# A graph layer with an on-chip sort: the first layer's exponential taken in two ScalarE passes, and four smaller moves

## The chip, the cores and the metric

The kernel runs on one core of a Trainium2 chip. The metric is the device time of one execution in microseconds (us). Three runs of the kernel before took 552.17, 550.02 and 552.18 us; their median is 552.17 us.

## The reference

`x` is 50,000 nodes by 128 features, with 12,500 edges (`src`, `dst`, 128 attributes each), all float32.

```python
edge_sum = segment_sum(edge_attr, src, 50000)
inputs   = concatenate([x, edge_sum], axis=1)        # 256 wide
h = elu(inputs @ W0 + b0)
h = elu(h @ W2 + b2)
out = h @ W3 + b3
return layernorm(x + out)                            # no scale, no shift
```

Only nodes that are the source of an edge have a nonzero `edge_sum`. The second half of `W0` matters for them alone.

## The kernel before, in words

**Items.** The nodes are worked on in 124 items, four blocks of up to 128 columns each. 98 dense items take all nodes in order (512 columns) as if they had no edges. 25 edge items (500 columns) and a last one (100) compute again the nodes that have edges, and their rows are scattered over the dense rows in `out`. Items 0 to 49 are dense, then one edge item and two dense ones take turns; the last six items are dense 118, edge 119 (group 23), dense 120 and 121, edge 122 (group 24) and the last one, 123.

**Steps.** Each engine's program is written out by hand as one loop over steps c = 0, 1, 2, ...; an engine runs its own list in order and waits on semaphores. In step c the engines work on several items at once:

- TensorE (PE): `layer1` of item c-1 (line 600, into `l1_ps`), `layer2` of item c-3 (L636), `layer3` of item c-5 (L646 and L647, eight products into one of three `z_ps`). `layer3` waits until the item three before it has left `z_ps`.
- ScalarE (ACT): `exp` of item c-1 (L720, `e1`), `turned`, which copies item c-1's x with a bias into `xT` (L713), `exp` of item c-3 (L720, `e2`), `squares` of item c-5 (L733, eight instructions), and for the second item of each pair in `ROOTS` a logarithm and an exponential that give `seed` (L741, L743).
- VectorE (DVE): `scale` (three small instructions on the root of a pair, L989 to L994), `first_layer` (the elu of item c-1), `output` (L1011, the normalised rows, seven steps after an item's number), `second_layer` (the elu of item c-3, L978 and L980).
- SyncE (SP) loads x and stores dense rows; GpSimd (POOL) issues the indirect DMAs: 100 that fetch x rows by edge (L441), 100 that gather edges in sorted order (L451), 100 that scatter edge rows (L470) and one for the last item (L494).

**The sort.** In steps 1 to 31 VectorE also sorts the edges by source: a bitonic network on a 128 by 128 tile `net`, in 31 groups of 2 to 5 operations, one group a step (`sort_group`). A compare is two instructions (L869, L870). Fourteen groups begin with the tile turned over by TensorE (`turn_net`, L532); these are steps 8, 9, 11, 12, 14, 15, 17, 18, 20, 22, 24, 26, 28 and 30, called turned steps here. `turn_net` waits for the last operation of the group before (`net_done`), and the group's first operation waits for the turned tile. The function `run(parts, beside)` deals the group's operations out between the step's parts: part, piece beside, part, piece beside, and what is left at the end.

**The bias on TensorE.** In steps 4 to 31 (`fused`) a third product (`add_bias`, L585) adds b0 + 1 to `l1_ps`, from three bf16 rows of b0 + 1 (`bias_rows`) against a row of ones. VectorE then needs one instruction for the elu, L974, `max(min(e1, 1), l1_ps)`, instead of two (L978, L980). The rows are made in steps 2 and 3 by `split_b0` (VectorE, from L820), `turn_b0` (TensorE, L527) and a cast (L833); TensorE and ScalarE wait for `bias_rows_ready` before step 4.

**After the sort.** `sorted_keys` (step 33), `targets` (step 34) and `keep_target` (step 35) on VectorE, with `turn_words`, `row_keys` and `turn_target` (L551) on TensorE, make the keys, the masks' inputs and the scatter's targets. From step 48 on edge groups are summed on TensorE.

## Time and profile before

| | |
|---|---|
| median of three runs | 552.17 us (550.02 to 552.18) |
| the profiled execution, whole | 550.06 us |
| its span in the profile | 547.9 us (2.2 us lie around it) |
| PE busy | 511.9 us, 93% |
| VectorE busy | 464.0 us, 85% |
| ScalarE busy | 409.2 us, 75% |
| GpSimd busy | 371.8 us, 68% |
| mean granted TensorE clock | 0.984 of 2.4 GHz |

The share of an engine is an average over the sort (up to 140 us), the sort's aftermath (to 161 us), a long stretch in which only the layers and the edge sums run, and a tail of scatters. A matmul's busy time in the records overlaps the next one's, so starts are compared here, not durations. Times in the timeline are counted from the start of the span.

### The profile page before, as it was taken

How to read it: one execution, taken by the hardware profiler on the slowest of the kernel's cores; microseconds unless marked ns; L12 is line 12 of the kernel's file. 1: busy time of each engine (PE TensorE's matmuls, PEld its weight loads, DVE VectorE, ACT ScalarE, POOL GpSimd, SP SyncE). 2: the span in 40 equal slices, each digit the busy share in tenths (PEclk: the TensorE clock that was granted, in tenths of full speed). 3: DMA queues.
4: the chain of work that ended last, by engine and by line, in shares of the span. 5: the costliest groups of instructions: out<-in, count | busy, mean ns of one | idle time of the engine just before them, and what ended most of it. 6: DMA issues, size and time to landing. Idle time of an engine off the chain costs nothing.

```text
span 547.9 us, 10022 instructions
## 1 busy us (share of the span) xinstructions
PE 511.9 (93%) x2895; PEld 362.3 (66%) x2895; DVE 464.0 (85%) x1215; ACT 409.2 (75%) x1510; POOL 371.8 (68%) x311
## 2 busy tenths in 40 slices
PE   6799999999979999999999999999999999999980
PEld 3356665566757767777777777777777777777670
DVE  8889898888999998898888989888889888888771
ACT  4377777777869878787787777777877877877760
POOL 6777778877730877778887878777677543333355
PEclk9799999999999999999999999999999999999996
DMA  5678989887667887766666665554445444332122
GB/s 164 189 208 262 282 255 269 260 257 228 195 179 253 246 224 207 212 198 180 197 192 187 181 182 172 150 157 134 130 131 151 125 136 117 96 101 89 56 68 64
DMA packets 87756, 96.98 MB, mean 177 GB/s; under 512 B 26403, under 2 KB 56595, under 8 KB 87703
## 3 DMA queue, kind: packets, MB, share of 16 engines
q1 hardware_dynamic: 58375, 70.67, 41.3%
q0 software_dynamic: 28896, 25.29, 19.0%
q8 instruction: 24, 0.39, 0.3%
q10 hardware_dynamic: 432, 0.39, 0.3%
q14 instruction: 29, 0.24, 0.1%
HBM read 58.10 MB, written 45.04 MB: 188 GB/s over the span
## 4 chain that ended last, share of the span: by engine, by line
PE 71%; DVE 18%; ACT 4%; issue 4%; POOL 1%; DMA 1%; POOLq 0%; DVEq 0%
PE z_ps L646 16%; PE z_ps L647 16%; PE l_ps L636 15%; PE l_ps L600 14%; PE side_ps L562 4%; DVE h L980 4%; PE l_ps L611 4%; DVE e L978 3%; ACT sq L733 3%; DVE o_sb L1011 2%; PE side_ps L628 2%; DVE net L869 2%; DVE net L870 1%; POOL out_dram L470 1%; DVE same L943 1%
## 5 line engine op out<-in xcount | busy, mean ns | idle before, releaser
L646 PE MATMUL z_ps<-center,xT 128*128 128x128 f32 (+1 forms) x986 | 190.2, 275 | 2.1 <-DVE o_sb L1011 2.1
L647 PE MATMUL z_ps<-w3c,h 128*128 128x128 f32 (+1 forms) x986 | 190.1, 275 | 0.0
L646 PEld LDWEIGHTS z_ps<-center,xT 128*128 128x128 f32 (+1 forms) x986 | 156.2, 191 | 48.0 <-issue 45.8
L733 ACT ACTIVATE sq<-z_ps 128x128 f32<-128x128 f32 (+1 forms) x493 | 129.4, 278 | 75.2 <-PE z_ps L647 74.8
L470 POOL DMA_INDIRECT out_dram<-pair_edge,target_i x100 | 121.6, 1216 | 87.2 <-issue 86.6
L451 POOL DMA_INDIRECT pair_edge<-pairs_dram,edge_i x100 | 124.5, 1245 | 51.3 <-issue 29.9
L647 PEld LDWEIGHTS z_ps<-w3c,h 128*128 128x128 f32 (+1 forms) x986 | 149.0, 191 | 0.0
L441 POOL DMA_INDIRECT x_early<-in_x_dram,src_i x100 | 122.4, 1224 | 32.6 <-issue 29.9
L636 PE MATMUL l_ps<-h,w 128*128 128x512 f32 (+1 forms) x248 | 128.3, 599 | 0.0
L720 ACT ACTIVATE e<-l_ps,bias 128x512 f32<-128x512 f32 (+1 forms) x150 | 102.2, 682 | 26.2 <-PE l_ps L636 19.8
L980 DVE SCALAR_TENSOR_TENSOR h<-l_ps,neg_bias,e 128x512 f32<-128x512 f32 (+1 forms) x150 | 111.2, 741 | 5.3
L600 PE MATMUL l_ps<-x_sb,w0x 128*128 128x512 f32 x196 | 102.0, 602 | 3.5 <-DVE bias_rows L833 3.2
L733 ACT ACTIVATION_READ_ACCUMULATOR sq<-z_ps 128x1 f32 (+1 forms) x493 | 102.8, 209 | 0.0
L978 DVE TENSOR_SCALAR e<-e,bias 128x512 f32<-128x512 f32 (+1 forms) x150 | 79.1, 528 | 1.6 <-ACT e L720 1.5
L713 ACT ACTIVATE xT<-x_sb,bias_x 128x512 f32<-128x512 f32 x98 | 70.9, 724 | 1.1 <-DVE bias_x L817 1.1
L1011 DVE TENSOR_TENSOR o_sb<-z_ps,rstd 128x512 f32<-128x512 f32 x98 | 66.8, 682 | 0.1
L636 PEld LDWEIGHTS l_ps<-h,w 128*128 128x128 f32 x248 | 41.1, 192 | 23.4 <-issue 21.8
L980 DVE SCALAR_TENSOR_TENSOR h<-l_ps,neg_b,e 128x512 f32<-128x512 f32 x70 | 52.6, 751 | 2.5
L720 ACT ACTIVATE e<-l_ps,b_in 128x512 f32<-128x512 f32 x70 | 48.3, 690 | 7.3 <-PE l_ps L600 6.0
L978 DVE TENSOR_SCALAR e<-e,b_in 128x512 f32<-128x512 f32 x70 | 38.7, 553 | 13.6 <-ACT e L720 13.0
L562 PEld LDWEIGHTS side_ps<-same,pair_edge 125*128 125x128 f32 x200 | 30.6, 191 | 25.3 <-issue 21.3
L989 DVE SCALAR_TENSOR_TENSOR newton<-seed 128x8 f32<-128x8 f32 (+2 forms) x63 | 11.2, 178 | 35.8 <-ACT seed L743 35.8
(140 smaller groups left out, 448.9 us busy)
## 6 DMA issues: line engine op xcount, KB each, us to landing
out_dram<-o_sb SPq DMA_DIRECT2D x98, 256.0 KB, 3.6
x_sb<-x_items_dram SPq DMA_DIRECT2D x97, 256.0 KB, 3.8
pairs_dram<-x_early SPq DMA_DIRECT2D x25, 250.0 KB
keyB<-key_rows_dram SPq DMA_DIRECT2D x25, 250.0 KB, 4.1
pairs_dram<-in_edge_attr_dram SPq DMA_DIRECT2D x24, 256.0 KB
x_early<-in_x_dram,src_i POOLq DMA_INDIRECT x100, 5.0
pair_edge<-pairs_dram,edge_i POOLq DMA_INDIRECT x100, 4.6
out_dram<-pair_edge,target_i POOLq DMA_INDIRECT x100
```

Source lines behind the costliest of these rows:

```text
L441: nc.gpsimd.indirect_dma_start(out=x_early[0:EP, k, j, :], out_offset=None, in_=x[:, :], in_offset=bass.IndirectOffsetOnAxis(ap=src_i[0:EP ...
L451: nc.gpsimd.indirect_dma_start(out=pair_edge[0:EP, c, :], out_offset=None, in_=pairs[:, :], in_offset=bass.IndirectOffsetOnAxis(ap=edge_i[ ...
L470: nc.gpsimd.indirect_dma_start(out=out[:, :], out_offset=bass.IndirectOffsetOnAxis(ap=target_i[0:EP, c:c + 1], axis=0), in_=pair_edge[0:EP ...
L600: mm = T.matmul(ps, w0x[:], x_in, start=True, stop=alone)
L636: T.matmul(l2_ps[c % 2][:, 0:n], w2[:], h1[:, c % H, 0:n], start=True, stop=True).then_inc(l2_ready, 1)
L646: T.matmul(z, xT[:, c % X, j * q:(j + 1) * q], center[:], start=True, stop=False)
L647: mm = T.matmul(z, h2[:, c % H, j * q:(j + 1) * q], w3c[:], start=False, stop=True)
L720: A.activation(e[:, c % 2, 0:n], ps[:, 0:n], ACT.Exp, bias=bias[:, 0:1]).then_inc(done, 1)
L733: t = A.activation(sq[0:q, c % 2, j, :], z_ps[c % Z][0:q, j * P:(j + 1) * P], ACT.Square, scale=float(P) ** -0.5, accum_out=ssq[0:q, r % R ...
L978: V.tensor_scalar(e[:, c % 2, 0:n], e[:, c % 2, 0:n], 1.0, bias[:, 0:1], ALU.min, ALU.add).then_inc(min_ready, 1)
L980: V.scalar_tensor_tensor(out=h[:, c % H, 0:n], in0=ps[:, 0:n], scalar=neg_bias[:, 0:1], in1=e[:, c % 2, 0:n], op0=ALU.max, op1=ALU.add).th ...
L1011: V.tensor_tensor(rows_out, z_ps[c % Z][0:q, 0:b * P].rearrange("p (j f) -> p j f", j=b), rstd[0:q, r % 2, at:at + b].rearrange("p (j a) - ...
```

## The change

1. **No bias product.** `add_bias`, `split_b0`, `turn_b0`, the cast and the constants for them go. TensorE no longer waits ahead of step 4; a wait for `bias1_ready` stands ahead of step 7.
2. **Two passes on ScalarE.** In steps 1 to 31 (`spared`) `below` writes r = relu(-l1 - b0) to `e1`, then comes the copy `turned`, then `exp_below` writes exp(-r) over it. VectorE takes one instruction, `elu_above`: max(l1 + (b0 + 1), e1). So items 0 to 2, which took two instructions on VectorE, take one, too.
3. **Turns later.** `turn_net` stands behind `layer2` instead of behind `layer1`, and in turned steps the group's first sort operation stands behind `first_layer`.
4. **`turn_target`** and `keep_target` move from step 35 to step 36.
5. **The tail.** The last six items have a root each (`ALONE`) and so go out six steps after their number, not seven. For edge group 23, too, each scatter waits for the dense rows that it alone needs.

```diff
-    ROOTS = [(c, c + 1) for c in range(0, NI - 2, 2)] + [(NI - 2,), (NI - 1,)]
+    ALONE = 6
+    ROOTS = [(c, c + 1) for c in range(0, NI - ALONE, 2)] + [(c,) for c in range(NI - ALONE, NI)]
...
-            return FUSED_FROM <= s < KEY_AT
+            return s < KEY_AT
...
-                    if g == NE - 1:
+                    if g >= NE - 2:
                         may_scatter(c)
...
-            def add_bias(ps, n, done):
-                T.matmul(ps, bias_rows[0:3, :], ones_row[0:3, 0:n], start=False, stop=True).then_inc(done, 1)
...
-                if c == FUSED_FROM:
-                    pe.wait_ge(consts_made, 5)
-                    pe.wait_ge(bias_rows_ready, 1)
+                if c == 7:
+
+                    pe.wait_ge(bias1_ready, 1)
...
-                elif c == 3:
-                    beside = [lambda: None, turn_b0]
                 elif c - SORT_AT in TURNED:
-                    beside = [lambda: turn_net(TURNED.index(c - SORT_AT))]
+                    beside = [lambda: None, lambda: turn_net(TURNED.index(c - SORT_AT))]
...
-                elif c == KEY_AT + 3:
+                elif c == KEY_AT + 4:
                     beside = [lambda: None, lambda: None, turn_target]
...
+            def below(c, ps):
+
+                act.wait_ge(l1_ready, c + 1)
+                A.activation(e1[:, c % 2, :], ps[:, :], ACT.Relu, bias=neg_b0[:, 0:1], scale=-1.0).then_inc(below_ready, 1)
+
+            def exp_below(c):
+                act.wait_ge(below_ready, c + 1)
+                A.activation(e1[:, c % 2, :], e1[:, c % 2, :], ACT.Exp, scale=-1.0).then_inc(exp1_ready, 1)
...
+                if c == 1:
+                    act.wait_ge(neg_b0_ready, 1)
...
                 for n in copies:
                     parts.append(lambda n=n: turned(n))
+                if item_in(c - 1) and spared(c):
+                    parts.append(lambda: exp_below(c - 1))
...
-            def split_b0():
-                link(V.tensor_scalar(bias_rest[:], b_in[:, 0:1], 1.0, None, ALU.add))
...
-                V.tensor_copy(bias_rows[0:3, :], z_ps[2][0:3, P:2 * P]).then_inc(bias_rows_ready, 1)
...
+            def elu_above(c, ps):
+
+                dve.wait_ge(exp1_ready, c + 1)
+
+                V.scalar_tensor_tensor(out=h1[:, c % H, :], in0=ps[:, :], scalar=b0_plus[:, 0:1], in1=e1[:, c % 2, :],
+                                       op0=ALU.add, op1=ALU.max).then_inc(h1_ready, 1)
...
-                    beside = sort_group(c - SORT_AT)
+
+                    beside = [lambda: None] * (c - SORT_AT in TURNED) + sort_group(c - SORT_AT)
```

**TensorE, turned step 20** (the first rows are the end of `layer3` in step 19, the last one the first product of `layer3` in step 20). Before:

```order
L646 MATMUL z_ps1<-center,xT 128x128
L647 MATMUL z_ps1<-w3c,h2 128x128
L600 MATMUL l1_ps1<-x_sb,w0x 128x512
L585 MATMUL l1_ps1<-ones_row,bias_rows 128x512
L532 MATMUL side_ps<-ident,net 128x128
L636 MATMUL l2_ps1<-h1,w2 128x512
L646 MATMUL z_ps2<-center,xT 128x128
```

and with the change:

```order
L632 MATMUL z_ps1<-center,xT 128x128
L633 MATMUL z_ps1<-w3c,h2 128x128
L588 MATMUL l1_ps1<-x_sb,w0x 128x512
L622 MATMUL l2_ps1<-h1,w2 128x512
L524 MATMUL side_ps<-ident,net 128x128
L632 MATMUL z_ps2<-center,xT 128x128
```

The bias product is gone, and the turn stands between the second and the third layer.

**ScalarE, one step of the sort with a root** (`e1` is the first layer's exponential, `e2` the second's). Before:

```order
L720 ACTIVATE e1<-l1_ps1,minus_one 128x512
L713 ACTIVATE xT<-x_sb,bias_x 128x512
L720 ACTIVATE e2<-l2_ps1,bias2 128x512
L733 ACTIVATE sq,ssq<-z_ps2 128x128 x4
L741 ACTIVATE seed<-ssq,eps 128x8
L743 ACTIVATE seed<-seed 128x8
```

and with the change:

```order
L709 ACTIVATE e1<-l1_ps1,neg_b0 128x512
L697 ACTIVATE xT<-x_sb,bias_x 128x512
L713 ACTIVATE e1<-e1 128x512
L704 ACTIVATE e2<-l2_ps1,bias2 128x512
L726 ACTIVATE sq,ssq<-z_ps0 128x128 x4
L734 ACTIVATE seed<-ssq,eps 128x8
L736 ACTIVATE seed<-seed 128x8
```

VectorE's elu of the first layer now waits for the third instruction of the step, not for the first.

**VectorE, a turned step of the sort whose group begins with a copy of the turned tile.** Before:

```order
L877 COPY net<-side_ps 128x128
L974 SCALAR_TENSOR_TENSOR h1<-e1,l1_ps1 128x512
L869 TENSOR_TENSOR net<-net 128x64
L870 TENSOR_TENSOR net<-net 128x64
L1011 TENSOR_TENSOR o_sb<-z_ps0,rstd 128x512
L869 TENSOR_TENSOR net<-net 128x2x32
L870 TENSOR_TENSOR net<-net 128x2x32
L978 TENSOR_SCALAR e2<-e2,bias2 128x512
L980 SCALAR_TENSOR_TENSOR h2<-l2_ps1,neg_bias2,e2 128x512
L869 TENSOR_TENSOR net<-net 128x4x16
L870 TENSOR_TENSOR net<-net 128x4x16
```

and with the change:

```order
L963 SCALAR_TENSOR_TENSOR h1<-l1_ps1,b0_plus,e1 128x512
L867 COPY net<-side_ps 128x128
L1004 TENSOR_TENSOR o_sb<-z_ps0,rstd 128x512
L859 TENSOR_TENSOR net<-net 128x64
L860 TENSOR_TENSOR net<-net 128x64
L971 TENSOR_SCALAR e2<-e2,bias2 128x512
L973 SCALAR_TENSOR_TENSOR h2<-l2_ps1,neg_bias2,e2 128x512
L859 TENSOR_TENSOR net<-net 128x2x32
L860 TENSOR_TENSOR net<-net 128x2x32
L859 TENSOR_TENSOR net<-net 128x4x16
L860 TENSOR_TENSOR net<-net 128x4x16
```

Each sort operation of the step stands one place later; the first one no longer keeps the elu waiting for the turn.

## Rows read from the trace of the kernel before

**Rows 1.** Windows: busy time of each engine, clock, DMA share, GB/s; mid-sort

```profile
75.00:100.00 25.00, 23.88 (x129) 15.24 (x127) 21.62 (x74) 18.44 (x70) 20.12 (x17) 1.00 0.91 273
```

**Rows 2.** Timeline of TensorE: a turned step (20), then a plain one (21)

```profile
87.96 0.33 PE L532 MATMUL side_ps<-ident,net 128*128 128x128 f32 x1 [0.67 <-DVE net L870]
88.12 1.03 PE L636 MATMUL l_ps<-h,w 128*128 128x512 f32 x2
88.99 0.39 PE L646 MATMUL z_ps<-center,xT 128*128 128x128 f32 x2
...
90.78 1.02 PE L600 MATMUL l_ps<-x_sb,w0x 128*128 128x512 f32 x2
...
94.80 1.02 PE L600 MATMUL l_ps<-x_sb,w0x 128*128 128x512 f32 x2
```

**Rows 3.** Timeline of TensorE: step 32, the first without a bias product

```profile
137.69 1.02 PE L600 MATMUL l_ps<-x_sb,w0x 128*128 128x512 f32 x2
...
141.20 1.02 PE L600 MATMUL l_ps<-x_sb,w0x 128*128 128x512 f32 x2
```

**Rows 4.** Timeline of ScalarE: step 19, and the squares of two steps later

```profile
82.13 0.28 ACT L733 ACTIVATE sq<-z_ps 128x128 f32<-128x128 f32 x1 [1.10 <-PE z_ps L647]
...
83.75 0.67 ACT L720 ACTIVATE e<-l_ps,minus_one 128x512 f32<-128x512 f32 x1
84.32 0.71 ACT L713 ACTIVATE xT<-x_sb,bias_x 128x512 f32<-128x512 f32 x1
84.93 0.67 ACT L720 ACTIVATE e<-l_ps,bias 128x512 f32<-128x512 f32 x1
...
90.98 0.28 ACT L733 ACTIVATE sq<-z_ps 128x128 f32<-128x128 f32 x1 [1.10 <-PE z_ps L647]
```

**Rows 5.** Timeline of VectorE: step 19, its elu and its last sort instruction

```profile
84.63 0.68 DVE L974 SCALAR_TENSOR_TENSOR h<-e,l_ps 128x512 f32<-128x512 f32 x1
...
87.68 0.22 DVE L870 TENSOR_TENSOR net<-net 128x64 f32<-128x64 f32 x1
```

**Rows 6.** Groups by line and form: busy us, mean ns, idle before them

```profile
L980 DVE SCALAR_TENSOR_TENSOR h<-l_ps,neg_b,e 128x512 f32<-128x512 f32 x70 | 52.6, 751 | 2.5
...
L741 ACT ACTIVATE seed<-ssq,eps 128x8 f32<-128x8 f32 x61 | 18.3, 301 | 2.0
...
L743 ACT ACTIVATE seed<-seed 128x8 f32<-128x8 f32 x61 | 12.7, 209 | 1.9
```

**Rows 7.** Timeline of VectorE: steps 2 to 8

```profile
12.37 0.14 DVE L820 TENSOR_SCALAR bias_rest<-b_in 128x1 f32<-128x1 f32 x1
...
13.88 0.15 DVE L827 CAST bias_parts<-bias_low 128x1 f32<-128x1 bf16 x1
...
20.91 0.69 DVE L974 SCALAR_TENSOR_TENSOR h<-e,l_ps 128x512 f32<-128x512 f32 x1 [1.04 <-ACT e L720]
...
22.82 0.49 DVE L978 TENSOR_SCALAR e<-e,bias 128x512 f32<-128x512 f32 x1 [0.56 <-ACT e L720]
...
36.43 0.29 DVE L874 TENSOR_TENSOR net<-side_ps,flips 128x128 int32<-128x128 int32 x1 [0.42 <-PE side_ps L532]
```

**Rows 8.** Windows, columns as in Rows 1: the start, and the pause after the sort

```profile
15.00:22.00 7.00, 4.48 (x6) 1.54 (x7) 5.71 (x23) 1.30 (x2) 5.70 (x5) 0.51 0.60 162
...
153.00:156.00 3.00, 0.24 (x3) 0.05 (x1) 2.83 (x15) 1.14 (x8) 2.39 (x3) 1.00 0.85 258
```

**Rows 9.** Timeline of TensorE: the end of step 35, and layer 3 of step 36

```profile
156.47 0.32 PE L551 MATMUL side_ps<-ident,target 100*125 100x100 f32 x1 [3.22 <-DVE dense_need L930]
...
158.77 0.46 PE L646 MATMUL z_ps<-center,xT 128*128 128x128 f32 x2 [0.22 <-DVE o_sb L1011]
```

**Rows 10.** Timeline of the tail: edge group 23's rows, its first scatter, the last scatter

```profile
528.88 0.68 DVE L1011 TENSOR_TENSOR pair_edge<-z_ps,rstd 125x512 f32<-125x512 f32 x1
...
531.25 1.19 POOL L470 DMA_INDIRECT out_dram<-pair_edge,target_i  x1 [2.40 <-issue]
...
543.18 0.99 POOL L494 DMA_INDIRECT out_dram<-x_end,end_i  x1 [0.30 <-issue]
```

More of the change, by code:

```diff
@@ L522, in bias1_product @@
                 pe.wait_ge(bias_x_ready, 1)
-                T.matmul(z_ps[2][:, 0:1], w0x[:], bias_x[:], start=True, stop=True)
-            def turn_b0():
-                pe.wait_ge(parts_split, 1)
-                T.transpose(z_ps[2][0:3, P:2 * P], bias_parts[:], ident[:]).then_inc(setup_mm, 1)
+                T.matmul(z_ps[2][:, 0:1], w0x[:], bias_x[:], start=True, stop=True).then_inc(setup_mm, 1)
             def turn_net(n):
@@ L598, in layer1 @@
                 ps = l1_ps[c % 2][:, 0:n]
-                alone = is_dense(c) and not fused(s)
-                mm = T.matmul(ps, w0x[:], x_in, start=True, stop=alone)
-                if alone:
+                mm = T.matmul(ps, w0x[:], x_in, start=True, stop=is_dense(c))
+                if is_dense(c):
                     mm.then_inc(l1_ready, 1)
-                elif is_dense(c):
-                    add_bias(ps, n, l1_ready)
                 elif c == LAST:
```

60 lines of the change are left out of this document (24 added, 36 removed).

## The prediction

> **What bounds the kernel now.** I read the windows first, then the three compute engines' timelines step by step through the sort, then the waits at the start, behind the sort and in the tail. Times are of the profiled execution (550.06 us, span 547.9).
>
> In mid-sort no engine is full: of 25 us VectorE works 21.6, ScalarE 18.4, TensorE shows 23.9, with overlaps between its records [rows 1]. A plain step takes TensorE 4.02 us (90.78 to 94.80) [rows 2]; the first step without a bias product takes 3.51 [rows 3]. So the product costs 0.51 us a step, more than its own columns. A turned step behind a group of four sort operations takes longer: TensorE stood idle 0.67 us until VectorE's last operation [rows 2].
>
> That wait closes a loop over two steps. Step 19: TensorE's third layer is there at 82.13, where the squares begin; the root follows, the exponential starts at 83.75 and runs 0.67 [rows 4]; VectorE starts the elu at 84.63 and ends its last sort operation at 87.90 [rows 5]; the turn starts at 87.96, then the second layer (0.87 to the third) and the third (1.79), and at 90.78 step 21 begins [rows 2], its squares at 90.98 [rows 4]: 8.85 us for steps 19 and 20. Two steps without such a stall (21 and 22) take about 8.1, twice the 4.02 and a little for the turn. After the sort TensorE runs at its own pace of 3.51 a step [rows 3], so what is won up to there is kept. The tail is GpSimd's: from 531.25 to 543.18 it starts nine DMAs, 1.49 apart without a pause [rows 10].
>
> **The change part by part.**
>
> *The bias product goes:* -0.51 a step on TensorE, 28 times, -14.3 us at most. It only counts where TensorE sets the pace.
>
> *Two passes.* Relu from PSUM has the shape of the old exponential: the next instruction starts 0.57 later [rows 4]. The second pass reads SBUF like the copy, which takes 0.71 [rows 4], but with no bias operand; the two small seed instructions are 301 ns with one and 209 without [rows 6], so I take 0.63, and 0.53 to the next start. The squares and a root take 1.62 together (82.13 to 83.75) [rows 4], of which the root's two instructions are some 0.45 [rows 6]. ScalarE's plain step is then 0.57 (relu) + 0.61 (copy) + 0.53 (second pass) + 0.57 (second layer) + 1.17 (squares) = 3.45; two steps with one root between them take 7.35 instead of 6.3. For VectorE the result is ready 0.57 + 0.61 + 0.63 = 1.81 after the relu starts, where it was 0.67. In step 19 that is 83.75 + 1.81 + 0.03 = 85.6 instead of 84.63. The elu has the form of L980, 0.75 with a scalar from memory and PSUM first [rows 6], and not the 0.68 of L974 [rows 5]: +0.07.
>
> *Turns behind the second layer* give back 0.87. So the stalled pair becomes 8.85 + 0.96 + 0.07 - 0.87 = 9.0, **0.18 longer than before**. The two-step stretch without a stall falls from 8.1 to ScalarE's 7.35 to 7.5. I went through steps 9 to 31 with these durations and each group's size. Steps 9 to 18: single turned steps behind a short or already delayed group (9, 12, 15, 18) gain 0.3 to 0.45 each, pairs (10, 11) and (16, 17) lose 0.65 and 0.45, as no root hid the longer exponential there: -0.5 together. Steps 19 to the end of the sort: four stalled pairs +0.7, twice +0.27 for a VectorE still behind from the step before, twice -0.63, and +0.8 because the sort's last operation ends 7.0 after step 31 begins, by the chain above, where it was 6.2 (at 139.9; step 32 began at 137.69 [rows 3], step 31 a plain 4.0 earlier); less 0.15 that pair (29, 30) was slower before than the rule: +0.7. Together **+0.2**. The ends: -5 if ScalarE's passes hide and every step goes at its own 3.7 us; +14.8 if each of 13 turned steps pays the whole 1.14.
>
> *The start.* VectorE is the engine that sets the pace from 12.4 to the turn of step 8. Eleven small instructions from 12.37 to 13.95 go [rows 7]: -1.58; the cast: -0.18; item 2's elu in one instruction instead of two (0.67 for 1.18): -0.51; the waits of 1.04 and 0.56 for ScalarE [rows 7], which came from TensorE starting step 4 late and slow (half the clock from 15 to 22 us [rows 8]), go with it: -1.60. Against it the two passes for items 0 and 1 put VectorE 0.64 back, and four elus cost 0.07 more. Sum -2.95; VectorE had no further wait until the turned tile of step 8 [rows 7], so the turn of step 8 comes 2.95 earlier, and as the second layer stands ahead of it, step 9 begins 3.8 earlier.
>
> But TensorE runs ahead in those steps and then has nothing to do: by VectorE's chain its second layer of step 8 is over near 28.2, and the tile comes at 33.1, a gap of 4.9 us. Before, the clock stayed at full speed in a gap of 3.22 [rows 8, 9], and fell to half (15 to 22 us) in one of 5.8 with one small product in it [rows 8]. I take it as falling again: then the third layer of step 8 runs 1.8 and the turn 0.1 longer, **+1.9**. The Trainium skill ("TensorE: Matmul & The Clock Gate", Part 1) says the throttled clock is the default and activity releases it; the half clock in these rows agrees, and by that rule the +1.9 is paid.
>
> *Behind the sort.* `turn_target` held TensorE 3.22 us in step 35, yet layer 3 of step 36 then waited for VectorE's output as well [rows 9], which stands behind `targets`. From the sort's last operation to there everything is VectorE's, 19 us without a pause. The 3.22 turn into a wait for `z_ps` one step later: gain 0, loss the turn itself, **+0.15**. Bounds -0.2 and +0.3.
>
> *The tail.* Group 23's rows were ready at 529.56 and its first scatter started at 531.25 [rows 10]. With its own root the item needs no partner and goes a step earlier; but item 118's root now sits ahead in the same queues (0.55 on each), so the rows come at about 528.4: **-1.15**. Bounds 0 and -1.8. The scatters behind it keep their 1.49; group 24's rows (before at 534.8, now 534.3) are in time.
>
> **Sum:** -3.8 + 1.9 + 0.2 + 0.15 - 1.15 = **-2.7**, so 547.4 us. The profiled execution lies 2.1 below the median shown (552.17); against the median 547.4 is -4.8, against its own -2.7. I leave it at 547.4, between what the two would give.
>
> **The rivals.**
>
> *A, the clock holds* in the gap of step 8, or the gap is shorter: then the 1.9 is not paid, 545.5 us. For it: the gap of 3.22. Against it: 4.9 is nearer to 5.8.
>
> *B, no change:* the start gives only what it removes (1.58 + 0.18), since VectorE's head start ends in a wait elsewhere (roots of items 0 and 1, squares in ScalarE's fuller queue), and the pairs lose 0.1 each: about 550. For it: VectorE had a wait for ScalarE at every early step.
>
> *C, slower:* ScalarE becomes the bound. Its relu joins the queue ahead of copy and exponential, and in a turned step VectorE, TensorE and the squares then wait in turn; if each of 13 turned steps costs 0.6 more than I reckon, +7.8 and 555.2 us. It decides from 0.4 a turned step (5.5 us in all). For it: the elu's data come 1.14 later after the relu begins than they did, and of that only the move of the turn is given back. Against it: ScalarE was idle 1.10 before each squares [rows 4]. The Trainium skill ("ScalarE: Activation LUTs", Rules for kernel authors) says relu should be given to VectorE and not to ScalarE. No run here shows it; VectorE is the fuller engine in these rows, which speaks against the rule for this kernel.
>
> **How the numbers follow.** My case has 0.40, A 0.22, B 0.23, C 0.15. About 0.5% (2.75 us) is what a measurement of this kernel can tell from no change. My case and A against a median near 552 are faster by more than that (0.62), but if the kernel before comes out at 550 mine is just within it: I take 0.08 off. Faster 0.54, within 0.5% 0.31, slower 0.15. The range takes in A's early side with the bounds of the tail and of the passes (543.0) and B with the nearer part of C (553.5).
>
> **What would show it.** The turn of step 8 near 33 us and step 9 near 37, TensorE idle about 5 us before it, and half the clock there (A: full clock, step 9 near 35). Steps 19 and 20 together 9.0, steps 21 and 22 some 7.4. The second pass 0.63, the elu 0.75. The sort's last operation about 2 us earlier than at 139.9. No wait of TensorE for `dense_need`, and one of some 3.5 us for `o_sb` in step 36. 3.50 steps as before from there on, the first scatter of group 23 about 3 us earlier than 531.25 in all. I am wrong if stalled pairs exceed 9.4 (C), if VectorE waits for ScalarE between 17 and 30 us (B), or if stretches behind the sort change their pace.

## The result, and the profile after

The changed kernel takes 552.48 us (median of 20 runs, 548.73 to 558.70), the kernel before 550.44 us (20 runs, 548.49 to 552.94) on the same chip: a ratio of 1.0041, 95% interval 1.0021 to 1.0061. It is 2 us slower, and the forecast was 547.4 and faster. Medians here and below are over all runs of a kernel, while ratios and their intervals leave out runs more than 1.5% above its fastest. The profiled execution of the changed kernel took 552.06 us, its span is 550.3; the one before took 550.06 with 547.9.

The two spans differ by 2.4 us. Starts on TensorE and VectorE cut it into five pieces. First TensorE's timeline after: the turn and the start of step 9, two of the first layers that wait, steps 32 and 33, the turned words with step 34, and step 37.

```profile
32.65 0.33 PE L524 MATMUL side_ps<-ident,net 128*128 128x128 f32 x1 [2.89 <-DVE net L860]
34.61 1.02 PE L588 MATMUL l_ps<-x_sb,w0x 128*128 128x512 f32 x2
...
84.82 1.12 PE L588 MATMUL l_ps<-x_sb,w0x 128*128 128x512 f32 x2 [1.07 <-DMA x_sb<-x_items_dram]
...
135.70 1.02 PE L588 MATMUL l_ps<-x_sb,w0x 128*128 128x512 f32 x2
...
139.48 1.02 PE L588 MATMUL l_ps<-x_sb,w0x 128*128 128x512 f32 x2
...
148.32 0.53 PE L529 MATMUL side_ps<-ident,words 100*125 100x100 f32 x1 [5.01 <-DMA words<-word_rows_dram]
148.64 1.96 PE L588 MATMUL l_ps<-x_sb,w0x 128*128 128x512 f32 x2
...
164.15 1.05 PE L588 MATMUL l_ps<-x_sb,w0x 128*128 128x512 f32 x2
```

Step 33 lasts 9.16 us (139.48 to 148.64), with a wait of 5.01 for the sorted words. It took 3.69 before, with no wait there: the words were turned at 144.70. The wait cost the clock, too. From 148 to 152 us the granted clock was 0.50, and step 34 took 6.74 us where it had 4.67 (windows of the changed kernel, columns as in [rows 1]):

```profile
148.00:152.00 4.00, 3.68 (x5) 1.72 (x6) 2.18 (x8) 1.30 (x2) 3.15 (x3) 0.50 0.79 217
```

VectorE's last sort instruction stands at 139.08 now:

```profile
139.08 0.22 DVE L860 TENSOR_TENSOR net<-net 128x64 f32<-128x64 f32 x1
```

| piece | before | after | difference |
|---|---|---|---|
| to the start of step 9 | 38.88 | 34.61 | -4.27 |
| step 9 to the end of the sort's last operation | 100.99 | 104.69 | +3.70 |
| from there to the turned words | 4.83 | 9.02 | +4.19 |
| turned words to step 37 | 15.92 | 15.83 | -0.09 |
| step 37 to the last scatter's start | 382.56 | 381.39 | -1.17 |

The last piece by GpSimd's timeline, which answers to [rows 10]: group 23's first scatter and the last one.

```profile
533.51 1.19 POOL L466 DMA_INDIRECT out_dram<-pair_edge,target_i  x1 [1.95 <-SPq L369]
...
545.54 0.99 POOL L490 DMA_INDIRECT out_dram<-x_end,end_i  x1 [0.30 <-issue]
```

The pieces add up to +2.36. The start gave more than forecast and the tail what was forecast. The sort lost 3.7, the words 4.2. TensorE's waits say where to look (us in total, times, longest; 20 to 170 us), of the kernel before:

```profile
PE side_ps L532 <- DVE net L870: 5.7, 9, 0.9
PE side_ps L551 <- DVE dense_need L930: 3.2, 1, 3.2
PE side_ps L542 <- DVE end_next L899: 0.3, 1, 0.3
PE z_ps L646 <- DVE o_sb L1011: 0.2, 1, 0.2
```

and of the changed kernel:

```profile
PE side_ps L524 <- DVE net L860: 9.4, 8, 2.9
PE l_ps L588 <- DMA x_sb<-x_items_dram: 6.2, 7, 2.0
PE side_ps L529 <- DMA words<-word_rows_dram: 5.0, 1, 5.0
PE z_ps L632 <- DVE o_sb L1004: 1.4, 1, 1.4
```

Two waits are new, and both are for transfers that SyncE issues. Its rows around the end of the sort, before:

```profile
133.47 0.29 SPq L379 DMA_DIRECT2D pairs_dram<-x_early  x1
136.80 0.34 SPq L359 DMA_DIRECT2D x_sb<-x_items_dram  x1
137.96 0.34 SPq L366 DMA_DIRECT2D out_dram<-o_sb  x1
139.90 0.34 SPq L400 DMA_DIRECT2D word_rows_dram<-net  x1
142.83 0.29 SPq L402 DMA_DIRECT2D words<-word_rows_dram  x1
```

and after:

```profile
132.36 3.05 SPq L357 DMA_DIRECT2D x_sb<-x_items_dram  x1
135.46 0.48 SPq L364 DMA_DIRECT2D out_dram<-o_sb  x1
136.06 0.33 SPq L377 DMA_DIRECT2D pairs_dram<-x_early  x1
136.43 3.15 SPq L357 DMA_DIRECT2D x_sb<-x_items_dram  x1
139.62 0.61 SPq L364 DMA_DIRECT2D out_dram<-o_sb  x1
140.35 0.54 SPq L398 DMA_DIRECT2D word_rows_dram<-net  x1
146.36 0.29 SPq L400 DMA_DIRECT2D words<-word_rows_dram  x1
```

A load of x waits for the ScalarE copy that frees its buffer. The copies that belong to the last x load ahead of the words, before and after:

```profile
136.07 0.71 ACT L713 ACTIVATE xT<-x_sb,bias_x 128x512 f32<-128x512 f32 x1
...
134.59 0.71 ACT L697 ACTIVATE xT<-x_sb,bias_x 128x512 f32<-128x512 f32 x1
```

Before, this load went out 0.02 us after the end of its copy and 3.3 us after the transfer ahead of it, and its issue took 0.34 us. After, the buffer is free at 135.31, but SyncE comes to the load only at 136.43; it issues back to back, this load takes 3.15 us to issue, and all behind it in the queue waits. It is so in the whole sort: from 30 to 140 us, 17 of the 25 x loads of the kernel before start 0.02 us after their copy and none over 0.9 us, while in the changed kernel all 25 start 1.1 to 9.4 us after theirs. The words' store goes out 1.05 us after the last sort operation instead of 0.03, right behind a store of 256 KB, and is confirmed 6.01 us after its issue instead of 2.93. Those two make 4.10 of the 4.19. Added up over its rows, SyncE spends 0.66, 0.79, 0.76 and 0.35 of its time in issues in 30 to 60, 60 to 90, 90 to 120 and 120 to 140 us before, and 0.90, 0.93, 0.95 and 0.95 after.

The DMA engines' share tells less. The windows of the changed kernel, columns as in [rows 1]:

```profile
90.00:120.00 30.00, 27.05 (x146) 18.28 (x144) 26.41 (x90) 27.01 (x98) 21.90 (x19) 1.00 0.87 263
120.00:140.00 20.00, 17.35 (x101) 12.41 (x101) 17.50 (x58) 15.95 (x57) 15.12 (x14) 1.00 0.83 258
```

and of the kernel before:

```profile
90.00:120.00 30.00, 29.32 (x160) 19.01 (x159) 25.55 (x88) 22.82 (x85) 24.18 (x20) 1.00 0.90 268
120.00:140.00 20.00, 18.50 (x97) 11.56 (x96) 17.06 (x60) 15.18 (x58) 16.04 (x14) 1.00 0.78 228
```

Up to 120 us they were as busy before. In the last 20 us of the sort they move 258 GB/s instead of 228.

### The profile page after: what moved, and what is told of

Its sections match the earlier page's. It is cut to its first block, busy times and chain, and to the rows that moved or that the text cites. A ratio compares the mean times of both kernels' runs of the same rounds, so it can differ in the third digit from the quotient of the medians.

```text
span 550.3 us, 10007 instructions
## 1 busy us (share of the span) xinstructions
PE 508.4 (92%) x2866; PEld 365.3 (66%) x2866; DVE 462.6 (84%) x1209; ACT 423.8 (77%) x1545; POOL 371.6 (68%) x310
## 4 chain that ended last, share of the span: by engine, by line
PE 68%; DVE 13%; ACT 7%; DMA 7%; issue 3%; POOL 1%; POOLq 1%; SPq 0%; ACTq 0%
PE z_ps L632 15%; PE z_ps L633 15%; PE l_ps L588 14%; PE l_ps L622 13%; DMA x_sb<-x_items_dram 5%; PE side_ps L554 4%; PE l_ps L597 4%; DVE h L973 2%; ACT sq L726 2%; PE side_ps L614 2%; DVE e L971 2%; DVE net L859 2%; DVE o_sb L1004 2%; DVE net L860 1%; ACT xT L697 1%
## 5 line engine op out<-in xcount | busy, mean ns | idle before, releaser
L588 PE MATMUL l_ps<-x_sb,w0x 128*128 128x512 f32 x196 | 105.5, 621 | 6.5 <-DMA x_sb<-x_items_dram 6.2
L622 PEld LDWEIGHTS l_ps<-h,w 128*128 128x128 f32 x248 | 43.3, 193 | 36.4 <-issue 33.3
L973 DVE SCALAR_TENSOR_TENSOR h<-l_ps,neg_b,e 128x512 f32<-128x512 f32 x67 | 50.3, 751 | 2.4
L704 ACT ACTIVATE e<-l_ps,b_in 128x512 f32<-128x512 f32 x67 | 46.3, 691 | 6.1 <-PE l_ps L588 6.1
L971 DVE TENSOR_SCALAR e<-e,b_in 128x512 f32<-128x512 f32 x67 | 36.7, 548 | 14.5 <-ACT e L704 13.8
L588 PEld LDWEIGHTS l_ps<-x_sb,w0x 128*128 128x128 f32 x196 | 31.0, 198 | 10.1 <-DMA x_sb<-x_items_dram 7.9
```

Of the source, the lines that this page charges most:

```text
L588: mm = T.matmul(ps, w0x[:], x_in, start=True, stop=is_dense(c))
L622: T.matmul(l2_ps[c % 2][:, 0:n], w2[:], h1[:, c % H, 0:n], start=True, stop=True).then_inc(l2_ready, 1)
L704: A.activation(e[:, c % 2, 0:n], ps[:, 0:n], ACT.Exp, bias=bias[:, 0:1]).then_inc(done, 1)
L971: V.tensor_scalar(e[:, c % 2, 0:n], e[:, c % 2, 0:n], 1.0, bias[:, 0:1], ALU.min, ALU.add).then_inc(min_ready, 1)
L973: V.scalar_tensor_tensor(out=h[:, c % H, 0:n], in0=ps[:, 0:n], scalar=neg_bias[:, 0:1], in1=e[:, c % 2, 0:n], op0=ALU.max, op1=ALU.add).th ...
```

## The experiments

Eighteen kernels ran in five sets, each against the kernel before on the set's own chip. That chip's median of the kernel before is given with each set, since it went from 551 to 578 us: on the slower ones ScalarE and TensorE have single stalls of 1 to 4 us for which the trace names no semaphore of another engine, in kernels of both kinds. So ratios there have wide intervals, and one trace of each kernel is compared step by step; the kernel before has a trace only on the chip of the result. "Trip" below is from the issue of the words' store to the issue of their load.

### Set 1 (kernel before: 576.23 us)

The attribute copies, one in each of steps 2 to 26, go to steps 26 to 38 instead, two a step; once in the changed kernel and once in the kernel before.

```diff
-    PAIR_ATTR = {2 + g: g for g in range(NE)}
+    PAIR_ATTR = {s: [g for g in range(NE) if 26 + g // 2 == s] for s in range(26, 39)}
```

> The changed kernel, with the 25 edge attribute copies (256 KB each, DRAM to DRAM) moved from steps 2 to 26 into steps 26 to 38, two a step. Theory DMA: in steps 9 to 26 the DMA engines and SyncE's queue are what binds the changed kernel, so TensorE's waits for x_sb go there (7.9 us of weight loads waiting before) and steps 9 to 25 take 72.5 us or less where the changed kernel took 75.7. Theory chain (the longer exponential and the turns alone set those steps): they stay at 75 to 76. Behind step 26 both expect more transfers at once, so the whole may be slower; only the stage decides.

> The same move in the kernel before. Theory DMA: it had 0.2 us of waits for x_sb, so its steps 9 to 25 stay within 0.5 us of 72.9. Theory chain: the same. If it gained as much as the changed kernel, the load of the DMA engines would cost both alike and not explain the difference.

Measured: ratios 0.9982 (0.9939 to 1.0025) and 0.9994 (0.9954 to 1.0034). The waits for `x_sb` in the sort are gone in the changed kernel, and steps 21 and 22 took 7.56 us, where the result's trace had 8.87 with a wait of 1.14 behind them. But steps 9 to 25 took 74.6 us, which neither theory had (72.5 or less; 75 to 76), and 76.9 in the kernel before, far from its expected 72.9: both have stalls of this chip in them. And the copies now stand around the words: trips of 5.20 and 4.75, steps 33 of 10.13 and 11.54 us. It fits x loads that are late because of what shares their queue. Whole times tell nothing here.

The words ahead of step 31's x load:

```diff
+                if c == KEY_AT:
+                    load(c - 1 + AHEAD)
-                if item_in(c) and is_dense(c) and ITEMS[c][1] + AHEAD < ND:
+                if item_in(c) and is_dense(c) and ITEMS[c][1] + AHEAD < ND and c != KEY_AT - 1:
```

> The changed kernel; step 31's x load is issued in step 32, behind the round trip of the sorted words, instead of ahead of it. Theory queue (the words' store stands in SyncE's queue and in the DMA rings behind a 256 KB load whose issue took 3.15 us): the trip from the sort's last operation to the turned words falls from 9.0 us to 5 to 6.5, TensorE's wait for the words from 5.0 to 1 to 2 us, and the whole by 3 to 4 us. Theory distance (the trip is long because the DMA engines are loaded by everything in flight): it falls by less than 1.5 us and the whole by less than 1.

The median of its six runs is 576.33 us, that of the kernel before 576.23; the ratio of 0.9919 (0.9851 to 0.9986) rests on two of the six, so the expected gain of 3 to 4 us is not shown. The trace has what was expected of the words: trip 3.75, step 33 5.75 us, and 5.77 from the last sort operation to the turned words.

The tail's part alone, in the kernel before:

```diff
+    ALONE = 6
+    ROOTS = [(c, c + 1) for c in range(0, NI - ALONE, 2)] + [(c,) for c in range(NI - ALONE, NI)]
...
-                    if g == NE - 1:
+                    if g >= NE - 2:
```

> The kernel before, with only the tail of the change: roots of their own for the last six items, and group 23's scatters waiting one by one. My reckoning: first scatter of group 23 1.15 us earlier (1.56 behind its rows), the whole 1.15 us faster, as the changed kernel's end caught up 1.1 of its 3.5 us there. Rival: the extra roots delay the items before them, and nothing is gained (within 0.3).

Ratio 0.9958 (0.9927 to 0.999). The forecast's -1.15 of 550 would be 0.9979, inside the interval.

### Set 2 (kernel before: 558.78 us)

The changed kernel itself, the words first again, and five buffers for x with each load a step earlier from step 12 on, after and before:

```diff
-        x_sb = sb("x_sb", [P, SLOTS, J * P])
+        x_sb = sb("x_sb", [P, X_SLOTS, J * P])
...
+                if item_in(c) and is_dense(c):
+                    while loaded[0] < min(ND - 1, ITEMS[c][1] + (3 if c < 12 else 4)):
+                        loaded[0] += 1
+                        load(loaded[0])
```

> The changed kernel itself, beside the kernel before, as a base for the three runs of this set. Every theory: 1.5 to 2.5 us slower than the kernel before (ratio 1.003 to 1.005), step 33 about 9 us long with a wait of TensorE for the sorted words of 4 to 5 us, and 5 to 7 us of TensorE's waits for x_sb between 27 and 140 us. If the loss is only that of one chip, the ratio lies within 1.000 plus or minus 0.002 here.

> The changed kernel, but SyncE issues step 31's x load only behind the sorted words' store and load. Theory Q (the words' round trip stands behind an x load and a store in SyncE's queue, and TensorE waits it out): the store of the words goes out within 0.5 us of the sort's last operation, step 33 falls from 9.2 to about 5, and the time falls by 3.5 to 4.5 us against the changed kernel, so 1.5 to 2.5 below the kernel before. Rival L (the trip is long because the DMA engines are full, not because of the order in the queue): step 33 stays above 7.5 and the time falls by under 1.5. Rival X (the load that is held back is missed in step 33 or 34): TensorE waits there for x_sb as long as it waited for the words, under 1 us gained.

> The changed kernel, but with five buffers for x in place of four, and from step 12 on each x load issued one step earlier. Theory Q (the x loads are late, not too many: the queue issues them late): TensorE's 5 to 7 us of waits for x_sb in the sort go, pairs without a stall fall to 7.4 to 7.6, step 32 starts 2 to 2.5 us earlier than the changed kernel's 135.7, and the time falls by about 2 us against the changed kernel if step 33 keeps its 9.2. Rival B (the DMA engines are full from 30 to 140 us, so an earlier issue only lengthens the landing): the waits stay above 3 us in sum and the time changes by under 0.7. Rival S (ScalarE's longer chain sets the steps, the waits for x only fill slack): the waits go, step 32 starts within 0.7 of 135.7 and the time does not move.

> The kernel before, with the same five buffers for x and the same earlier loads. It waited only 0.2 us in all for x_sb. Theory Q and rival S: within 0.7 us of the kernel before. Rival B' (x loads limit the kernel before too, through the queue's order and the stores behind the loads): over 1.2 us faster.

Measured: 0.9972 (0.9930 to 1.0013), 1.0001 (0.9962 to 1.0040), 1.0002 (0.9966 to 1.0037) and 0.9989 (0.9949 to 1.0030). None can be told from no change. That holds for the changed kernel itself, too (median 557.79 against 558.78): its interval lies below that of the result, so the loss of 2 us was seen on one chip and not on this one, although the words came later still. Step 33 of the changed kernel took 12.47 us here, with a wait for the words of 8.5 and a trip of 6.19. Words first missed: the store went out 0.03 us after the last operation, but its trip was 6.66 and step 33 9.31. The transfer ahead had gone out 1.8 us earlier, as in runs with trips of 3.6; I have no reason for this one. With five buffers the waits for `x_sb` in the sort fell from 4.0 to 0.2 us, so they are a matter of when a load is issued and not of bytes alone; steps 21 and 22 took 7.40 us, as expected. Step 32 came at 139.34 against 137.09 and not 2 us earlier, as one turned step had a stall of 4 us that the trace ties to nothing.

### Set 3 (kernel before: 550.98 us)

This chip is like that of the result. The x loads of items 8 to 35 fetch 8 of 128 partitions in the first two kernels, whose computation for those items therefore runs on older rows:

```diff
-                sp.dma_start(x_sb[:, d % SLOTS, :], x_items[d * P:(d + 1) * P, :])
+                q = 8 if 8 <= d < 36 else P
+                sp.dma_start(x_sb[0:q, d % SLOTS, :], x_items[d * P:d * P + q, :])
```

> The changed kernel, but the x loads of items 8 to 35 fetch 8 of their 128 partitions (the rest of the buffer keeps older rows, so x of those items is left out). This takes about a quarter of the bytes off the DMA engines from 30 to 160 us and leaves every instruction of the compute engines. Theory Q (the changed kernel lost its gain in the DMA: late x loads and the sorted words' trip behind full queues): TensorE's waits for x_sb fall from 6 us to under 1, the words' store takes about 3 us to land instead of 6, step 33 goes from 9.2 to 4 to 5, the DMA share falls from 0.85 to under 0.75, and the time lies 4 to 8 us below the changed kernel's, so 2 to 6 below the kernel before. Rival S (ScalarE's longer chain sets the steps): step 33 shortens all the same, but steps 9 to 31 take their 101 us as in the changed kernel and the time falls by under 3.

> The kernel before with the same thin x loads for items 8 to 35. It waited 0.2 us for x_sb in all and its words' store took 2.9 us. Theory Q: within 1 us of the kernel before, so that with thin loads on both sides the change is worth about the forecast 2.7 us or more. Rival D (the DMA engines hold the kernel before as well, through the fetches and stores): it gains as much as the changed kernel does, over 3 us, and the difference of the two stays at 2 us to the changed kernel's disadvantage.

With thin loads the changed kernel takes 548.63 us, ratio 0.9953 (0.9935 to 0.9970); the kernel before 550.42, 0.9989 (0.9969 to 1.0010). The same bytes are worth 3.85 us to the one (552.48 less 548.63, across two chips whose kernels before differ by 0.5) and nothing that can be measured to the other. **With light x loads on both sides the change gains 1.8 us, where it loses 2.0 with full ones.** TensorE's waits in the thin changed kernel:

```profile
PE side_ps L525 <- DVE net L861: 17.0, 11, 2.9
PE side_ps L530 <- DMA words<-word_rows_dram: 3.7, 1, 3.7
PE z_ps L633 <- DVE o_sb L1005: 1.7, 1, 1.7
PE l_ps L589 <- DMA x_sb<-x_items_dram: 0.4, 1, 0.4
```

Its steps 9 to 31 take 98.62 us (35.59 to 134.21), against 101.09 in the changed kernel, 98.81 before and 98.43 in the thin kernel before: 2.5 us of the sort's loss come with full x loads, and what the change does to the engines' chain costs these steps 0.2 us in sum. Part of the 2.5 is clock: behind a wait of 1.96 us for x (at 70.88) the granted clock of the changed kernel was 0.50 from 72 to 74 us. Step 33 missed the expected 4 to 5 and took 7.79. SyncE's rows show why, and that an x load of 16 KB also takes 3.33 us to issue, so that what it waits for is not its own size:

```profile
133.83 3.33 SPq L358 DMA_DIRECT2D x_sb<-x_items_dram  x1
137.21 0.36 SPq L365 DMA_DIRECT2D out_dram<-o_sb  x1
137.80 0.55 SPq L399 DMA_DIRECT2D word_rows_dram<-net  x1
143.36 0.27 SPq L401 DMA_DIRECT2D words<-word_rows_dram  x1
```

The 256 KB store stands 0.59 us ahead of the words, and their trip is 5.56 us, while the DMA share from 120 to 140 us is only 0.55:

```profile
120.00:140.00 20.00, 18.27 (x104) 12.60 (x103) 17.13 (x56) 15.76 (x63) 15.95 (x14) 1.00 0.55 155
```

So full engines are not what makes this trip long. The thin kernel before has the store 1.98 us ahead and a trip of 2.63.

Then the attribute copies early, and that with five buffers and the words first:

```diff
-    PAIR_ATTR = {2 + g: g for g in range(NE)}
+    PAIR_ATTR = {s: [g for g in range(NE) if (2 + g // 2 if g < 12 else g - 4) == s] for s in range(2, 21)}
```

> The changed kernel, but the 25 copies of the edge attributes go out two a step in steps 2 to 7 and one a step in steps 8 to 20, so that none is left in steps 21 to 26. Theory Q in its form of bytes (what counts is how full the DMA engines are when the words go out): TensorE's waits for x_sb after step 21 go, but the early steps have more of them; the words' trip is still behind the x load of step 32, step 33 7 to 9; the time falls by 0 to 1.5 us. Rival: the copies at the start delay the x loads there, 1 us slower or more.

> The changed kernel with all three: five buffers for x with each load a step earlier from step 12 on, the words ahead of step 31's x load, the attribute copies in front. Theory Q: step 33 5 to 6, no waits for x_sb, 3 to 5 us below the changed kernel, 1 to 3 below the kernel before. If the DMA engines' bytes bind and not the order, 0 to 1.5 below the changed kernel.

Medians 551.93 and 550.90 us, ratios 0.9999 (0.9965 to 1.0034) and 1.0011 (0.9978 to 1.0044). With the copies in front alone the store of the rows stood 1.8 us ahead of the words, the trip was 3.55 and step 33 took 5.74 us. TensorE then waited 3.39 us for `o_sb` in step 36, which is what the forecast had, and its clock fell to half there and in two turned steps. The combination had no waits for x in the sort behind step 8 and a trip of 3.22, and was expected 1 to 3 us below the kernel before; it is not. Step 9 starts at 35.76 and 36.15 in the two, later than in the result (34.61), and step 37 22.1 and 22.2 us after the last sort operation, where the kernel before has 20.75: there the gain went.

### Set 4 (kernel before: 557.47 us)

The x load and the store of step 31 both behind the words; that with the copies in front; the tail alone again; and the changed kernel with the turns back ahead of the second layer.

```diff
+                if c == KEY_AT:
+                    load(c - 1 + AHEAD)
+                    store(c - 8)
+                    confirm(c - 10)
...
-                    beside = [lambda: None, lambda: turn_net(TURNED.index(c - SORT_AT))]
+                    beside = [lambda: turn_net(TURNED.index(c - SORT_AT))]
```

(the first hunk, with both left out of step 31, is that of the first two kernels, the last one that of the fourth)

> The changed kernel, but SyncE takes both the x load and the output store of step 31 behind the sorted words' store and load. In the changed kernel the store of step 31's rows went out 0.7 us ahead of the words, and the words took 6.0 us to land. Theory H (the words stand behind a 256 KB store and load in the same queue): the words land in 3 to 4 us, step 33 takes 5 to 6 instead of 9.2, step 37 starts 3 to 4 us earlier against the sort's last operation (it lay 24.9 behind it), and the time falls by 2.5 to 4 us against the changed kernel, 0.5 to 2 below the kernel before. Rival B (the DMA engines are full from all sources): they still take over 5, and nothing is gained.

> The same with the attribute copies done by step 20 (two a step in steps 2 to 7). Theory H with the late x loads gone as well: no waits for x_sb behind step 18, step 32 starts by 135.5, step 33 takes 5 to 6, and the time lies 2 to 4 us below the kernel before. Rival: the clock falls in step 8 and again in a turned step and in step 36, as it did in the run with copies in front, and takes 2 to 3 us of it back: 0 to 1 below the kernel before.

> The kernel before with the tail's part alone (own roots for the last six items, group 23's scatters each waiting for its own rows). Forecast -1.15 us; the changed kernel's trace gave 1.1 between step 37 and the end; an earlier run of this edit gave 0.9958. Expected 0.9965 to 0.9985. If it reaches 0.996 or less, the tail was worth more than forecast.

> The changed kernel with the turns back ahead of the second layer and the sort's first operation back ahead of the elu. By the forecast each stalled turned pair then takes 9.9 instead of 9.0, some eight turned steps pay 0.87, so 5 to 7 us later at the sort's end and 4 to 7 us slower than the changed kernel if nothing else moves. Rival: since the x loads are late and SyncE's queue is full, the slower sort gives the queue its time back, and the loss is under 2 us with the waits for x_sb gone.

Ratios 0.9975 (0.9939 to 1.0012), 0.9977 (0.9938 to 1.0017), 0.9977 (0.9936 to 1.0018) and 1.0159 (1.0092 to 1.0226). Trips 4.98, 4.20, 4.86 and 4.17, steps 33 of 7.18, 6.13, 5.39 and 6.05. The first two cannot be told from the kernel before. The first keeps the transfers of some 250 KB 4.5 us away from the words and has a trip of 4.98 all the same, where 3 to 4 was expected. The second was to start step 32 by 135.5 and starts it at 142.19: it has no waits for x behind step 18, as expected, but one of 3.34 us ahead of that, and stalls. The tail alone came out as expected. The fourth is clear: with the turns ahead of the second layer, steps 9 to 31 take 108.7 us (36.67 to 145.41) against 104.2 in the first (36.45 to 140.62). Two of the stalled pairs take 9.9, as expected, and two 11.5. It costs 8.9 us against the kernel before. The changed kernel itself did not run on this chip; if its other parts cost the 2 us of the result, some 6 to 7 go to the turns, and by the steps 4.6; 4 to 7 were expected. The turns' new place is worth about what the forecast said.

### Set 5 (kernel before: 578.24 us)

A 256 KB attribute copy from step 25 goes right ahead of the words in the kernel before, and the kernel with both held back runs again.

```diff
-    PAIR_ATTR = {2 + g: g for g in range(NE)}
+    PAIR_ATTR = {2 + g: g for g in range(NE) if g != 23}
...
                     sp.wait_ge(net_done, DONE[-1])
+                    pair_attr(23)
```

> The kernel before, except that one 256 KB copy of edge attributes, which went out in step 25, goes out in SyncE's queue right ahead of the sorted words' store. No byte and no instruction is added. Theory H (the words wait for what stands ahead of them in the queue, and all behind the sort waits for the words): the words' store takes 4.5 to 6 us instead of 2.9, TensorE waits 2 to 3 us for the words, step 37 starts 2 to 3 us later after the sort's last operation, and the time is 1.5 to 3 us longer (ratio 1.003 to 1.006), which is the size of the changed kernel's loss. Rival (the sort's aftermath has slack, TensorE's 3.2 us wait for dense_need takes it up): the words come later, step 37 does not, ratio 1.000 to 1.002.

> The changed kernel with SyncE's x load and output store of step 31 behind the words, run again. Theory H: the words' store lands in 3 to 4.5 us, step 33 takes 5 to 7 instead of 9.2, step 37 starts 22 to 23 us after the sort's last operation instead of 24.9, and the ratio to the kernel before is 0.995 to 1.000 where the changed kernel had 1.0041. Rival B (full DMA engines, whatever stands ahead): the store takes over 5 and the ratio stays above 1.002.

The whole times of this set do not carry a verdict. The 17 runs of the kernel before go from 568.77 to 585.15 us. The ratio for the kernel before with the copy is 1.0077 (1.0021 to 1.0133), but it rests on six of those 17, and over all runs its median is 577.36 against 578.24. So it is not shown that the copy makes the kernel slower. The trace shows the trip, 6.31 us:

```profile
147.49 2.29 SPq L359 DMA_DIRECT2D x_sb<-x_items_dram  x1
149.82 0.65 SPq L366 DMA_DIRECT2D out_dram<-o_sb  x1
150.58 0.55 SPq L384 DMA_DIRECT2D pairs_dram<-in_edge_attr_dram  x1
151.18 1.40 SPq L401 DMA_DIRECT2D word_rows_dram<-net  x1
157.49 0.28 SPq L403 DMA_DIRECT2D words<-word_rows_dram  x1
```

From the last sort operation (150.35) to the turned words (159.38) are 9.03 us, as the changed kernel had 9.02, and step 37 starts 23.4 us after that operation, where the kernel before had 20.75 on the chip of the result. So late words come in the kernel before as well, with none of the change's other parts there, and 2.65 of the 4.2 us reach step 37. But the first two rows show that on this chip an x load with a long issue and a 256 KB store stood right ahead of the copy, so the trace does not say what the copy alone did.

The kernel with both held back: median 571.93 us against 577.36 for the other kernel of the set and 578.24 for the kernel before. The ratio is 0.9868 (0.9819 to 0.9917), but the runs within 1.5% of each kernel's fastest differ in their means by only 0.1%, so a gain is not shown.

```profile
148.37 0.34 SPq L398 DMA_DIRECT2D word_rows_dram<-net  x1
151.25 0.28 SPq L400 DMA_DIRECT2D words<-word_rows_dram  x1
```

Trip 2.88, step 33 4.80, step 37 22.4 us behind the last sort operation instead of 24.85: the steps are as expected. How much of the time is the words' cannot be said; step 32 came at 144.84 against 148.26 in the other kernel of the set.

**All twenty traces together.** In the seven where a transfer of some 250 KB went out in the last 1.4 us ahead of the words' store, the trip is 4.75 to 6.31 us (the changed kernel 6.01, its repetition 6.19, thin after 5.56, late attributes 5.20 and 4.75, tail again 4.86, behind a copy 6.31). In the other thirteen it is 2.63 to 4.98, but for the one of 6.66. On the two faster chips the groups lie apart (5.56 and 6.01 against 2.63 to 3.55), on the slower ones they overlap, and 4.98 and 6.66 stand there without a transfer so close ahead. So the order in the queue is the likely cause of the long trip, and not the only one.

## Why the prediction was wrong

**The step that failed** is the one behind the sort: "From the sort's last operation to there everything is VectorE's, 19 us without a pause." That is true of the rows of the kernel before, where VectorE worked 18.1 of those 19 us. But the sorted words' round trip through DRAM runs beside that work with little slack, and the prediction had no term for it. From the sort's last operation to the turned words it grew from 4.83 to 9.02 us, and TensorE waited 5.01 for them.

The prediction followed the compute engines and did not ask whether SyncE can follow when buffers come free sooner. It could not: every x load went out late, the last one ahead of the words took 3.15 us to issue instead of 0.34, and the words' store went out 1.05 us after the last sort operation and right behind one of 256 KB. The kernel before had slack exactly there. That these transfers make the loss is shown, on the two chips that are alike, by the thin loads, with which the change gains 1.8 us. That within the trip it is the order in the queue is supported by the thin trip of 5.56 us at a DMA share of 0.55 and by the two groups of trips on the faster chips, and not proven. Nor does shortening the trip bring the forecast: the two kernels that did it on a chip like that of the result are equal to the kernel before.

**The sort, forecast +0.2, measured +3.70.** This is the second step that failed: the sum has no term for waits for x. TensorE's products had none in the kernel before (a weight load had 0.2 us) and 6.2 us in the changed one, and 2.5 us of the loss go away with thin loads. Most of it lies in steps 9 to 18, which take 45.47 us instead of 43.05. The remaining 1.2 are in the thin kernel too (step 9 to the last operation 102.18 against 100.99). Of that, +0.88 is the span from step 31's start to the last operation, 7.07 where it was 6.19; forecast 7.0 and 6.2. The rest is 0.3 in the steps before, where I had reckoned with -0.6.

**What was right.** The chain of engines, by its durations: in the changed kernel the second pass is 626 ns and the new elu 749 (0.63 and 0.75):

```profile
L963 DVE SCALAR_TENSOR_TENSOR h<-l_ps,b_plus,e 128x512 f32<-128x512 f32 x31 | 23.2, 749 | 13.5 <-ACT e L713 13.5
...
L713 ACT ACTIVATE e<-e 128x512 f32<-128x512 f32 x31 | 19.4, 626 | 0.0
```

Steps 19 and 20 take 9.05 us with full and 9.01 with thin loads (forecast 9.0), steps 21 and 22 7.56 with thin loads (7.4); the thin kernel's last sort operation ends 2.1 us earlier than in the kernel before (2.0), and 1.6 earlier than in the thin one. The tail gave 1.17, and 1.22 between the thin kernels (1.15).

**Right by luck.** Step 37 came 15.83 us after the words instead of 15.92, near the forecast's +0.15. But the forecast's path was not taken: TensorE ran step 34 at half its clock and waited 1.41 us for `o_sb` in step 36, not some 3.5. The forecast's wait is in the runs with copies in front (3.39), and there step 37 comes 16.3 us after the words, with the clock at about half in step 36.

**The start, forecast -3.8 + 1.9, measured -4.27.** The turn of step 8 came at 32.65 (33.1). The gap ahead of it was 2.89 us and not 4.9, as TensorE's second layer of step 8 ended near 29.75 and not 28.2, and the clock stayed at full speed through it: rival A's case. It need not. In two kernels of set 3 above TensorE waited as long, and the granted clock of the 2 us behind the turn was half. After, thin after, and copies in front, in that order (window 32 to 34 us):

```profile
32.00:34.00 2.00, 1.35 (x12) 1.36 (x13) 2.00 (x7) 0.00 (x0) 1.43 (x2) 1.00 0.60 142
```

```profile
32.00:34.00 2.00, 1.65 (x8) 1.66 (x9) 2.00 (x9) 0.00 (x0) 1.53 (x2) 0.50 0.55 158
```

```profile
32.00:34.00 2.00, 1.62 (x8) 1.62 (x9) 2.00 (x9) 0.00 (x0) 1.56 (x2) 0.50 0.79 233
```

From the turn to step 9 they take 3.24 and 3.38 us instead of 1.96. The 1.9 was a price of 1.3 to 1.4, paid in some executions. Against its own sum the start came 2.4 us better than forecast, which hid half of what the words cost: without the clock's luck the result would be further off. The page of the Trainium skill that the prediction weighed ("TensorE: Matmul & The Clock Gate", Part 1) has the half clock as the default from which activity releases; these rows agree that it is lost in a gap of this length, and show that it need not be.

**The rivals.** A's mechanism came true and its time did not. B named a wait elsewhere that swallows the start, which is what happened, but put it on ScalarE and in the first steps, and there the turn of step 8 came as early as the chain said. C did not happen: with thin loads the stalled pairs took 9.0 to 9.2, under the 9.4 at which it decides. The rule that it weighed from the Trainium skill ("ScalarE: Activation LUTs", Rules for kernel authors), relu to VectorE, was not tried, so no run here shows it. C's threshold is a little off (13 turned steps at 0.4 are 5.2 us, not 5.5), and so is the count of small instructions at the start (nine in the trace, not eleven, over the same 1.58 us); neither changes the sum. None of the three looked at SyncE, though the instruction behind every wait for x is its.

**What stays open.** The kernel with both transfers held back was not run on a chip like that of the result, so whether it beats the kernel before there is not shown; neither of its two sets can tell it from the kernel before safely. Nor is it shown why the result's loss did not come again in set 2, and what makes SyncE's issues long. The trip of 6.66 us with words first is unexplained, and so are the stalls on the slower chips.

## What to carry to other kernels

When a change makes the engines that free buffers faster, write down the order of the DMA queue around each round trip through DRAM that somebody waits for, with the gap ahead of it: here 1.9 us between a 256 KB store and the words went with a trip 3 us shorter than 0.7 us did, and nothing in the compute engines' timelines said so. Compare each load's issue with the moment its buffer comes free: when the issuer starts it microseconds later, the issuer is the bound, whatever the DMA engines' share says. A short, waited-for transfer can be put ahead of the bulk ones of its step by program order; here that shortened step 33 in most traces, and no run shows that it made the kernel faster for certain.

## What the runs showed of the hardware

- SyncE's issue of a 256 KB x load took 0.34 us when the transfer ahead was 3.3 us old, and anything from 0.34 to 4.8 us when it was younger, with no clear limit; a load of 16 KB took 3.33 us, too. These are not waits for a buffer, which in the changed kernel had been free for 1.1 us or more each time. I read it as the queue holding the instruction back until earlier transfers have made room, which no run measured by itself; 17 of 25 loads from 30 to 140 us took over 2 us in the changed kernel, 10 before.
- A store of 49 KB 0.6 to 0.7 us behind a 256 KB transfer in the same queue was confirmed after 5.6 to 6.3 us, and after 2.6 to 3.6 with nearly 2 us between them on the faster chips; on the slower ones nearly 2 us gave 3.5 to 6.7. The Trainium skill ("DMA: Bandwidth & Descriptors", Queues, rings and completion order) says that each DMA engine takes a queue's descriptors in order; the 6.01 us behind the 256 KB store agree with that.
- Equal waits do not mean equal clocks: after 2.86 and 2.96 us of waiting in step 8 TensorE came back at half speed, after 2.89 at full. In step 35 the kernel before waited 3.22 us and kept its clock, and its thin variant waited 3.21 and lost it, step 36 taking 6.43 us instead of 3.99. Shorter waits did the same: behind 1.96 us for x (at 70.88) in the changed kernel and 2.04 us for the turn (at 72.86) with copies in front the granted clock fell to 0.50, and behind 2.04 us in thin after it did not. So a pause of 2 to 3 us cost the clock in some executions and not in others, and up to 2.4 us of time.
